# Layer 0 of a two-layer recurrent model rewritten: expert products on gathered rows, fp32 attention scores over 32 rows, RMS norm in transposed layout

## The reference, cut to what matters

```python
# s: 16 heads of 16 features; 16 key blocks of 32 tokens per sequence
gate = einsum('bshd,bnhd->bhsn', q, km)      # km: mean key of a block; future blocks -1e30, own block +1e30
sel = top 4 blocks of gate                   # per token and head
scores = where(sel_tok & causal, q k^T * d**-0.5, -1e30)
o = softmax(scores) v
o = o * rsqrt(mean(o*o) + 1e-6) * o_norm_w   # RMS norm over a head's 16 features
s = o @ Wo.T
# g: 8 experts of 176 hidden units, the 2 best of each token, and one shared expert of 352 units
topk_w, topk_idx = top_k(softmax(x @ gate_w), 2)
g = silu(x w_gate[e]) * (x w_up[e])
routed = sum over the 2 experts of topk_w * (g w_down[e])
out = routed + (silu(x sw_gate) * (x sw_up)) sw_down
```

## Time and profile before

| | |
|---|---|
| time, median of 3 runs | 458.74 us (455.46 to 459.42) |
| span of the profiled execution, first to last instruction | 457.3 us |
| layer 0 / layer 1 in that span | 339.8 / 117.5 us |
| busy: TensorE (PE) / VectorE (DVE) / ScalarE (ACT) / GpSimd (POOL) | 77% / 68% / 39% / 43% |
| mean granted TensorE clock | 0.88 of full |
| moved by DMA | 30.2 MB |

### The profile page before, as it was taken

One profiled execution on the slowest core, in us unless ns is written; L12 is line 12 of the kernel. 1 busy time (PEld: TensorE's weight loads), 2 busy tenths in 40 slices (PEclk: granted clock), 3 DMA queues, 4 the chain that ended last, 5 costly groups with the idle time before them and its releaser, 6 DMA issues. The chain is left out here.

```text
span 457.3 us, 6207 instructions
## 1 busy us (share of the span) xinstructions
PE 351.9 (77%) x2088; PEld 254.3 (56%) x2088; DVE 313.0 (68%) x857; ACT 180.0 (39%) x319; POOL 196.9 (43%) x133
## 2 busy tenths in 40 slices
PE   0795785838508989999999999999656686994852
PEld 0584574725306656675666665666545574772742
DVE  4867699639408885888346664674769959859893
ACT  1312623602011422234445344544203675865720
POOL 5562652913213652536255536564354342304026
PEclk9998888859955998999999999999895979795895
DMA  8000299979890412212101141110015000000002
GB/s 272 28 26 7 95 136 181 135 204 124 171 107 23 114 37 44 71 34 75 39 36 36 58 140 36 36 34 1 2 54 189 1 1 0 0 1 1 0 0 92
DMA packets 23066, 30.20 MB, mean 66 GB/s; under 512 B 3171, under 2 KB 18187, under 8 KB 23035
## 3 DMA queue, kind: packets, MB, share of 16 engines
q1 hardware_dynamic: 19003, 18.80, 21.9%
q10 hardware_dynamic: 4032, 11.01, 7.8%
HBM read 24.99 MB, written 4.82 MB: 65 GB/s over the span
## 5 line engine op out<-in xcount | busy, mean ns | idle before, releaser
L380 POOL TENSOR_TENSOR wl<-wr,wh 128x768 fp32r<-128x768 f32 x28 | 51.3, 1833 | 76.7 <-ACT wh L466 60.4
L522 ACT ACTIVATE PT<-bank 128x512 f32<-128x512 f32 (+1 forms) x88 | 44.3, 557 | 39.5 <-PE bank L946 39.4
L679 DVE TENSOR_REDUCE mx<-bank 128x1 f32<-128x384 f32 (+3 forms) x88 | 52.3, 635 | 10.7 <-PE bank L927 10.4
L925 PE MATMUL bank<-KS,QS 112*128 112x128 bf16 (+3 forms) x128 | 34.5, 323 | 30.4 <-DVE mx L679 21.8
L149 PE MATMUL bank<-xh,wh 128*128 128x512 f32 x112 | 51.5, 460 | 4.0 <-DVE gb L804 1.4
L418 POOL TENSOR_TENSOR gl<-gb,gh 128x512 fp32r<-128x512 f32 x28 | 36.2, 1293 | 37.4 <-DVE gh L811 24.9
L790 DVE SCALAR_TENSOR_TENSOR s<-th,bank 128x512 f32<-128x512 f32 x28 | 19.2, 685 | 41.0 <-ACT th L529 41.0
L150 PE MATMUL bank<-xl,wh 128*128 128x512 f32 x112 | 46.3, 413 | 0.0
L151 PE MATMUL bank<-xh,wl 128*128 128x512 f32 x112 | 46.2, 413 | 0.0
L925 PEld LDWEIGHTS bank<-KS,QS 112*128 112x128 bf16 x128 | 13.0, 103 | 46.8 <-DVE mx L679 32.1
L149 PE MATMUL bank<-wh,gh 128*128 128x256 f32 x112 | 37.6, 335 | 0.5 <-POOL gl L418 0.5
(11 more groups left out here) (249 smaller groups left out, 924.0 us busy)
## 6 DMA issues: line engine op xcount, KB each, us to landing
wr<-in_w_chunks_dram ACTq DMA_DIRECT2D x28, 384.0 KB, 3.2
QS<-parts_dram SPq DMA_DIRECT2D x12, 256.0 KB
KS<-parts_dram SPq DMA_DIRECT2D x12, 256.0 KB, 9.3
parts_dram<-wp SPq DMA_DIRECT2D x4, 384.0 KB, 3.5
parts_dram<-x SPq DMA_DIRECT2D x4, 384.0 KB, 15.3
acts<-in_w_ai_dram SPq DMA_DIRECT2D x1, 1152.0 KB, 6.4
x<-in_x_dram SPq DMA_DIRECT2D x2, 512.0 KB, 6.4
KS<-in_x_dram SPq DMA_DIRECT2D x1, 1024.0 KB, 5.6
```

The lines of the kernel that those rows point to most:

```text
L380: pool.tensor_tensor(wl[:, s % 3, :, :], wr[:, s % 2, :, :], wh[:, s % 3, :, :].bitcast(F32), ALU.subtract).then_inc(wl_ready, 1)
L522: act.activation(PT[:, k % 8, 0:n], bank[k % 2][:, 0:n], ACT.Exp, scale=float(DH) ** -0.5).then_inc(P_ready, 1)
L679: dve.tensor_reduce(mx[:, b * TB + i, heads[0]:heads[-1] + 1], bank[k % 2][:, 0:len(heads) * n].rearrange("p (h n) -> p h n", n=n), AX.X, ...
L925: pe.matmul(out, QS[0:R_MAX, h, b * S + i * P:b * S + (i + 1) * P], KS[0:R_MAX, h, b * S:b * S + n], start=True, stop=False)
```

## The change

All of layer 0 is rewritten; layer 1 is the same line for line.

- **Experts.** The shared expert stays dense, with split products on gate and up (items SG) and plain fp32 products for its down side (SD). The routed experts run on gathered rows. DVE ranks the 2048 token-expert pairs (`rank_out`, on 16 small products of PE, item RK), so that each expert's rows stand together, padded to tiles of 128 rows: 23 tiles at most, always 23. POOL writes the normalized rows to their places in DRAM with 16 indirect DMAs. Each tile j is four items: M1 transposes its rows; M2 multiplies by gate and up of its expert (2 fp32 products of 352 columns), with ACT's tanh and two DVE products; M3 transposes the hidden rows back; M4 is the down product (2 of 256 columns). ACT copies its result out, SP writes it to DRAM. At the end POOL gathers each token's two rows with 16 indirect DMAs (item GA), and DVE adds them with their weights (MZ).
- **Expert weights.** SP first copies the weights within DRAM to a layout by expert. Then, for each tile, it loads the tile's expert number from SBUF into a register and issues three transfers from addresses that depend on it, into one of three buffers `w` (536 KB a tile).
- **Scores.** Heads lie 32 rows apart: 16 features and 16 rows for the block mask. A score is one fp32 product over 32 rows, two heads at a time from two row groups of the array (SA by query for the maxima, SB by key), each with the causal bf16 product of before. Nothing of q, k, mask or maxima goes through DRAM; PE transposes them (KT, QT) and ACT copies them. PSUM is used as a ring of two pairs of banks.
- **RMS norm** in transposed layout: PE sums the squares (RS), POOL takes the power and spreads it, PE transposes it (RT), DVE multiplies. Wo is 32 fp32 products at the end (WO).
- **Order.** One list of items, `ORDER`, is walked by PE, DVE, ACT and POOL alike. `weave` merges attention and experts by estimated costs.

```diff
+def program_order():
+    head = [("QK", t) for t in range(TB)] + [("RO", 0), ("RO", 1), ("RK",), ("RO", 2), ("RO", 3)]
...
+    attention += weave([("QK", 6), ("RO", 6), ("QK", 7), ("RO", 7)] + prepare(1), by_query(0))
+    attention += [("QT", 0, 0, 2), ("QT", 0, 1, 2)]
+    attention += weave(by_key(0), by_query(1))
+    attention += [("QT", 1, 0, 2), ("QT", 1, 1, 2)]
+    attention += by_key(1)
+    experts = []
+    for n in range(B):
+        experts += [("SG", n, c) for c in range(SCH)] + [("SD", n, k) for k in range(2)]
+    for s in range(NT + 3):
+        experts += [(f"M{k + 1}", s - k) for k in range(4) if 0 <= s - k < NT]
+    experts += [("GA", t) for t in range(T)] + [("MZ", b) for b in range(B)]
+    order = head + weave(attention, experts)
+    return order + [("WO", b) for b in range(B)]
...
         @block.sync
         def _(sp):
...
+            def expert_in(j):
+                if j >= 3:
+                    sp.wait_ge(Y_ready, j - 2)
+                e = sp.value_load(eid[0:1, j:j + 1], min_val=0, max_val=E - 1)
+                sp.dma_start(w[:, j % 3, 0:KD * GU].rearrange("p (s n) -> p s n", n=EH),
+                             wide_dram[:, :, bass.ds(e * EH, EH)].rearrange("s p n -> p s n")).then_inc(w_in[j % 3], 16)
+                o = KD * GU
+                sp.dma_start(w[:, j % 3, o:o + D], down_dram[bass.ds(e * EH, P), :]).then_inc(w_in[j % 3], 16)
+                sp.dma_start(w[0:E2, j % 3, o + D:o + 2 * D], down_dram[bass.ds(e * EH + P, E2), :]).then_inc(w_in[j % 3], 16)
...
+            for j in range(NT):
+                if j + 4 < NT:
+                    rows_in(j + 4)
+                sp.wait_ge(y_read, j + 1)
+                sp.dma_start(yg_dram[j * P:(j + 1) * P, :], ysb[:, j % 2, :]).then_inc(y_out[j % 2], 16)
+                if j + 3 < NT:
+                    expert_in(j + 3)
...
+                if kind == "M2":
+                    j = item[1]
+                    pe.wait_ge(w_in[j % 3], 48 * (j // 3 + 1))
+                    pe.wait_ge(xgT_read, j + 1)
+                    if j:
+                        pe.wait_ge(mg_ready, j)
+                    for k in range(KD):
+                        ins = pe.matmul(GUb[:, 0:GU], xgT[:, j % 2, k * P:(k + 1) * P], w[:, j % 3, k * GU:(k + 1) * GU],
+                                        start=(k == 0), stop=(k == KD - 1))
+                    ins.then_inc(GU_ready, 1)
...
+                if kind == "M4":
...
+                    pe.matmul(out, mgT[:, j % 2, 0:P], w[:, j % 3, o:o + D], start=True, stop=False)
+                    pe.matmul(out, mgT[0:E2, j % 2, P:2 * P], w[0:E2, j % 3, o + D:o + 2 * D], start=False,
+                              stop=True).then_inc(Y_ready, 1)
```

More of the change, by code:

```diff
@@ L62 @@
 OW = N_SEL * H_SEL + N_SEL
[L65 to L111, removed]
 def spread(ap, axis, n):
@@ L151, in split_matmul, with weave, cost @@
     return pe.matmul(out, l_lo, r_hi, start=False, stop=stop, skip_group_check=skip)
+NT = (T * P * EK) // P + E - 1
+GU = 2 * EH
+WROW = KD * GU + 2 * D
+E2 = EH - P
+RING_ENGINE = {"RK": "dve", "KT": "act", "QT": "act", "GT": "act", "SA": "dve", "SB": "act", "RS": "dve", "RT": "dve",
+               "WO": "dve"}
+def weave(first, second):
+    def cost(item):
+        return ITEM_COST.get(item[0], 0.0)
+    total = [sum(cost(i) for i in s) for s in (first, second)]
+    done, at, out = [0.0, 0.0], [0, 0], []
+    while at[0] < len(first) or at[1] < len(second):
+        if at[1] >= len(second) or (at[0] < len(first) and done[0] / total[0] <= done[1] / total[1]):
+            k = 0
+        else:
+            k = 1
+        item = (first, second)[k][at[k]]
+        out.append(item)
+        done[k] += cost(item)
+        at[k] += 1
+    return out
@@ L175, in layer0 @@
[L175 to L190, removed]
+        strict = m.sb("strict", [P, P], BF16)
@@ new lines, in _ @@
+            for k in range(KD):
+                for side in range(2):
+                    sp.dma_start(wide_dram[2 * k + side].rearrange("p (c n) -> p c n", n=P),
+                                 chunks[0:ECH, :, k, side * P:(side + 1) * P].rearrange("c p n -> p c n")
+                                 ).then_inc(relaid, 16)
+            sp.dma_start(down_dram.rearrange("(c p) d -> c p d", p=P), chunks[0:ECH, :, KD, :]).then_inc(relaid, 16)
+            sp.wait_ge(zero_ready, 1)
+            sp.dma_start(xg_dram.rearrange("(j p) d -> p j d", p=P), spread(ysb[:, 0, :], 1, NT)).then_inc(cleared, 16)
@@ L456, in values @@
+            for t in range(TB, T):
+                act.copy(Z[:, t, 0, :, DH:2 * DH], spread(onehot[:, t % TB, :], 1, H)).then_inc(z_init_q, 1)
+            act.wait_ge(sw_in, 16)
+            act.copy(swl[:, 0], sw).then_inc(swh_ready, 1)
+            act.wait_ge(v_init, 1)
+            for t in range(T):
                 act.wait_ge(vg_ready, t + 1)
-                act.wait_ge(init_done, 1)
-                vg = bank[6 + t % 2]
-                act.copy(V[:, t, :, 0:DH], vg[:, 0:D].rearrange("p (h d) -> p h d", d=DH))
+                vg = bank[4 + t % 4]
@@ new lines, in _ @@
+            dve.tensor_tensor(rt[:, 0, :, :], lg[:, :, :], spread(rm[:, 0, :], 2, E), ALU.subtract).then_inc(e_in, 1)
+            dve.wait_ge(e_out, 1)
+            dve.wait_ge(pads_init, 1)
+            link(dve.tensor_reduce(rm[:, 1, :], rt[:, 1, :, :], AX.X, ALU.add))
+            link(dve.reciprocal(rm[:, 2, :], rm[:, 1, :]))
+            link(dve.tensor_tensor(sc[:, :, 0:E], rt[:, 1, :, :], spread(rm[:, 2, :], 2, E), ALU.mult))
+            for t in range(T):
+                ins = dve.max(rtop[:, t, :], sc[:, t, :])
```

1469 lines of the change are left out of this document (733 added, 736 removed).

## The result

The changed kernel takes 689.84 us (median of 4 runs, 687.02 to 695.32), the kernel before 457.1 us beside it: 1.516 times as long, 95% interval 1.505 to 1.527. I had predicted 513 us, range 440 to 590. The direction was right, the size far off: a loss of 233 us, not of 54.

What follows compares the result with a forecast made beforehand. PE's product stream was taken to bound the last half of layer 0 before the change. Stages of 48 + 107 + 203 + 36 + 117.5 gave 511.5, with 1.4 over the span 513 us, 12% slower; range 440 to 590.

Steps and rivals of the forecast that it cites:

- Stage A: Layer 0 from its start to the end of routing, on DVE: 48 us (44 to 54).
- Stage B: Preparation and maxima of sequence 0, before tile 0: 75 us on DVE plus 32 of chains, 107 us.
- tile 0 near 200: Sign that the term before tile 0 failed, by chains between engines or scatters; tile 0 was forecast at 155 us.
- Stage C: The 23 tiles: weights' round trip sets a period of 9.5 us (6.5 to 13), 203 us in all.
- The trip without M4: In the tiles, from M4's end through copy, write, register load and weight transfers to the waiting M2: 5.9 us.
- 3.0 us behind the weights: In each tile, PE's items from M2 of tile j+3 until M4 of tile j+1: 3.0 us (2 to 4.5).
- the sum of 511.5: The whole kernel's span: 48 + 107 + 203 + 36 + 117.5 us, against the profiled 457.3 before.
- 0.85 ns a column: Price of an fp32 product on PE at the full clock, against 0.46 for split products.
- Pairing: Attention scores: two heads side by side cost 0.27 plus 0.12 us an item, one after the other 0.54 plus 0.12.
- Rival 4: In the tiles, PE's idle time halves the clock, period 11 to 12: 550 us; above 550, with rival 3 in part, 0.15.
- Stage D: The tail of layer 0, from last PV through 16 gathers to the final sums: 36 us (24 to 66).
- rival 3: Indirect DMAs cost 3 us each, exposing gathers and delaying rotations: 559 us; chance 0.15, shared with Rival 4 in part.

Runs made afterwards that it cites:

- e5: The changed kernel with M4 put first in each step of the experts' order, nothing left out: 605.51 us.
- e8: The changed kernel with the expert steps in the order M1, M4, M2, M3, nothing left out: 602.38 us.

## Why the prediction was right or wrong

- **Stage A:** right, 48 against 50.
- **Stage B, 107 against 153: wrong.** The step that failed is "PE has some 50 us here, so it doesn't bound". It was busy 112.8, at a clock of 0.75. Its groups from 49 to 203 us, and DVE waiting for it:

```profile
L940 PE MATMUL S<-kT,qT 32*128 32x128 f32 (+3 forms) x136 | 33.6, 574 | 0.6 <-ACT kT L565 0.3 <-issue 0.2
...
L1023 PE MATMUL bank<-sdn,sg 128*128 128x256 f32 x48 | 16.2, 506 | 0.0
...
L943 PE MATMUL S<-tri,ident_b 128*128 128x128 bf16 x68 | 10.6, 242 | 0.0
L771 DVE TENSOR_REDUCE mx<-S 128x2 f32<-128x256 f32 (+3 forms) x34 | 27.2, 801 | 49.7 <-PE S L943 49.3
```

  34 items cost (33.6 + 10.6) / 34 = 1.3 us, not 0.40. DVE's own sum was right: 73.0 us busy against 75. I had put only chains of 32 us on top of it, and did not price the stage by each engine. The sign I gave for this stage, tile 0 near 200, came, but it named the chains or the scatters as the cause; DVE's largest wait here was for PE's scores.
- **Stage C, 203 against 322: the mechanism right, its size wrong.** The trip without M4 was put at 5.9 and came out at 5.4 to 6.0 in all tiles but one. The terms that failed are M4, 0.6 against 2.2, and "3.0 us behind the weights" against 8.8. At the full clock these are 1.2 (264.82 to 265.98) and 4.7 us: that much is the second pass and my thin count of items. The rest, 5 us in a tile that runs at half clock, is the clock. The forecast "PE waits some 4 us, about 20 times" became 2.0 us, 18 times, because the longer run of items covered more of the trip. Stages B and C make 46 and 119 of the 174 us by which the profiled span missed the sum of 511.5.
- **The source of the price.** I took 0.85 ns a column from the row of eight transposes and called them fp32 products. A transpose is one record. The doubled records of true fp32 products stood in the trace of before as well: the eight records of PV are four products. The Trainium skill (FP8 and Floating Point Precision, TensorE Precision Notes) states that true fp32 takes four passes through the array; 1.78 ns here against 0.46 for fp32r is 3.9 times, so the runs agree. With these terms as they are at the full clock, stage C would have had a period of 4.7 + 1.2 + 5.9 = 11.8 us instead of 9.5, some 45 us more: 560 us, still 130 short.
- **Pairing.** I took a pair as half of two. At the full clock, a pair of 256 columns over 32 rows (weights loaded once), and two in a row over 128 (four tiles, all rows):

```profile
265.98 0.70 PE L949 MATMUL S<-qT,kT 32*128 32x256 f32 x4
266.61 0.29 PE L952 MATMUL S<-tri,ident_b 128*128 128x128 bf16 x2
```

```profile
262.64 1.10 PE L943 MATMUL S<-kT,qT 128*128 128x256 f32 x4 [0.22 <-issue]
263.58 0.28 PE L946 MATMUL S<-tri,ident_b 128*128 128x128 bf16 x2
```

  0.63 against 0.94 us: a third less, not a half. Two of 256 columns over the same 32 rows, one by one at the full clock, start 1.06 us ahead of what follows (115.07 to 116.13, four tiles, same rows): against these the pair saves two fifths. The two do run side by side, as the Trainium skill (TensorE: Matmul & The Clock Gate, Part 3) has it, but the gain is smaller than a half, and the clock took it back.
- **Rival 4** (the clock falls) named what decided, at 550 us; it failed by the same price and by holding the fall for a matter of idle time only. The Trainium skill (TensorE: Matmul & The Clock Gate, HAM oscillation — how this bites in real kernels) tells of a loop whose DMA waits bring the clock down in every turn. The runs with and without weight waits agree, 0.64 against 0.80 (M4 first) and 0.90 (loads made once); but the four-tile kernel, at 98.6% busy and 0.60 and with a fall 25 us after the last wait over 0.2 us, shows that waits are not the whole of it.
- **Stage D, 36 against 44:** sixteen gathers start 1.25 us apart, 1.2 predicted, so rival 3 is out. Most of the 8 us stands behind the last gather: from its landing (554.7, where DVE's last adds start) to the end of the layer 14.6 us pass, where I had 9.5. Some 3 us of it lie between POOL's last sum and layer 1; what makes the rest was not tried.
- **What the change does after all.** Of 233 us, the kernel with four tiles shows 142 (133 by its fastest execution); the other 19 tiles add 91 to 100. Even without the round trip the changed kernel is 113 us slower than before. The DRAM stacks that it did away with had bought one record and 112 to 115 rows for each score.

## What to carry to other kernels

Price a product by its number of records and the distance between starts, for the very type and form, and sum the work of each engine in each stage before saying that it doesn't bind. A prefetch is worth the distance in the order between the last reader of a buffer and its next: count the items there, since moving one entry of the order was worth 84 us here. Before a product is cut into narrow row groups, look at what the granted clock does: here half the columns at half the clock were no gain.

## What the runs showed of the hardware

- 32-row fp32 products at 98.6% busy left the clock at 0.60 (and from 350 to 400 us, busy 50.00 of 50 us, at 0.50), where 128-row products at 90.9% busy had 0.97. In the four-tile kernel the clock fell from 1.00 to 0.50 at 252 us, 5 us after the last tile's M4 and 25 us after the last wait over 0.2 us. Once at full clock, the same 32-row items with 128-row tiles between them and no waits stayed at 0.99 for 100 us.
- Eighteen waits of 2 us on a DMA went together with 82 us beyond their own 36.9, by the run without them (and without the transfers).
- The register load in a DMA's address cost 0.27 us and its arithmetic 0.15, where I had put 0.9; an indirect DMA of 128 rows of 1 KB 0.95 on POOL and 0.30 to the next.
- Two of the changed kernels scatter more than the one before: 593 to 607 us (e5) and 600 to 649 (e8) in equal executions, against 453 to 462. What decides between them was not tried.
